# Writing out ScalarE's and VectorE's programs for the middle experts in a mixture-of-experts kernel

## The reference

```python
# x: (128, 64, 256), cond: (128, 256), weight: (256, 256), w1: (8, 256, 1024), w2: (8, 1024, 256)
ys = cond * scale
d = rsqrt(einsum('bi,io->bo', ys * ys, weight * weight) + EPS)
hidden = einsum('bsi,io->bso', x * ys[:, None, :], weight) * d[:, None, :]
logits = hidden @ wr.T                                # 8192 x 8
vals, idx = top_k(logits, 2); gating = softmax of the two
# the first 2560 tokens of each expert are kept, in order (cap)
h = gelu(einsum('ecd,edf->ecf', hidden[dispatch], w1) + b1)
y = einsum('ecf,efd->ecd', h, w2) + b2
out = x + segment_sum(y * gate, token)
```

## Time and profile before

| | |
|---|---|
| median of 3 runs | 928.7 us (927.84 to 929.36) |
| the profiled execution's own time | 929.16 us |
| its span, first to last instruction | 927.0 us |
| busy: TensorE | 903.6 us, 97% of the span |
| busy: ScalarE, VectorE, GpSimd | 543.0, 486.7, 436.4 us |
| mean granted TensorE clock | 0.992 of full speed |

### The profile page before, as it was taken

The page is one execution under the profiler, slowest core; times in us unless marked ns, Lnnn a source line. Parts: engine busy times, 40 slices in busy tenths (PEclk is TensorE's granted clock), DMA queues, the critical chain, the costliest instruction groups (busy, mean ns, idle before and its releaser), DMA issues.

```text
span 927.0 us, 20314 instructions
## 1 busy us (share of the span) xinstructions
PE 903.6 (97%) x6627; PEld 866.5 (93%) x6627; DVE 486.7 (52%) x1166; ACT 543.0 (59%) x1292; POOL 436.4 (47%) x472
## 2 busy tenths in 40 slices
PE   9999999999999999989999999989999999999995
PEld 6666799999999999989999999989999999999995
DVE  6589867546455554435444554435444644544442
ACT  4888655646566665656556665655566655664552
POOL 0000324555466555654446645654466544674453
PEclk9999999999999999999999999999999999999998
DMA  9675492543523353333523442333334231342232
GB/s 344 230 251 185 154 314 36 95 95 48 130 46 59 53 138 46 52 60 45 132 39 50 69 125 46 61 55 94 73 52 60 52 51 29 57 66 40 47 46 25
DMA packets 56119, 84.53 MB, mean 91 GB/s; under 512 B 6848, under 2 KB 45264, under 8 KB 55664
## 3 DMA queue, kind: packets, MB, share of 16 engines
q0 software_dynamic: 28592, 38.20, 26.9%
q1 hardware_dynamic: 25760, 44.87, 14.2%
q10 hardware_dynamic: 1696, 0.58, 0.2%
HBM read 53.71 MB, written 38.31 MB: 99 GB/s over the span
## 4 chain that ended last, share of the span: by engine, by line
PE 92%; issue 3%; ACT 2%; DVE 2%; DVEq 0%; ACTq 0%; POOLq 0%; POOL 0%
PE bank L609 13%; PE bank L623 13%; PE bank L625 13%; PE bank L626 13%; PE bank L610 13%; PE bank L611 13%; PE bank L512 5%; PE bank L597 3%; PE bank L525 2%; PE bank L527 1%; PE bank L560 1%; PE bank L492 1%; ACT sb_x L755 0%; ACT sb_h_hi L823 0%; ACT sb_hid_t L791 0%
## 5 line engine op out<-in xcount | busy, mean ns | idle before, releaser
L823 ACT ACTIVATE sb_h_raw<-bank,sb_b_now 128x384 f32<-128x384 f32 (+1 forms) x416 | 223.4, 537 | 257.6 <-PE bank L611 240.1
L1232 DVE TENSOR_TENSOR sb_h_lo<-sb_h_raw,sb_h_hi 128x384 fp32r<-128x384 f32 (+1 forms) x416 | 213.3, 513 | 280.5 <-ACT sb_h_hi L823 264.6
L623 PE MATMUL bank<-sb_w_hi,sb_h_hi 128*128 128x256 f32 x1064 | 305.2, 287 | 1.2 <-DVE sb_h_lo L1232 1.2
L436 POOL DMA_INDIRECT out_rows<-sb_y,sb_add_ids x154 | 254.2, 1650 | 102.0 <-issue 51.8
L625 PE MATMUL bank<-sb_w_lo,sb_h_hi 128*128 128x256 f32 x1064 | 300.2, 282 | 0.0
L626 PE MATMUL bank<-sb_w_hi,sb_h_lo 128*128 128x256 f32 x1064 | 298.9, 281 | 0.0
L609 PE MATMUL bank<-sb_xt_hi,sb_w_hi 128*128 128x384 f32 (+1 forms) x832 | 265.9, 320 | 7.7 <-ACT sb_h_hi L823 7.7
L611 PE MATMUL bank<-sb_xt_hi,sb_w_lo 128*128 128x384 f32 (+1 forms) x832 | 261.8, 315 | 0.0
L610 PE MATMUL bank<-sb_xt_lo,sb_w_hi 128*128 128x384 f32 (+1 forms) x832 | 261.7, 315 | 0.0
L823 ACT ACTIVATE sb_h_hi<-bank,sb_b_now 128x384 fp32r<-128x384 f32 (+1 forms) x416 | 220.9, 531 | 0.0
L623 PEld LDWEIGHTS bank<-sb_w_hi,sb_h_hi 128*128 128x128 f32 x1064 | 200.8, 189 | 2.1 <-DVE sb_h_lo L1232 2.1
(11 more groups left out here) (144 smaller groups left out, 582.5 us busy)
## 6 DMA issues: line engine op xcount, KB each, us to landing
sb_w_raw<-in_w SPq DMA_DIRECT2D x16, 1024.0 KB
hidden<-sb_rows SPq DMA_DIRECT2D x4, 2112.0 KB, 9.5
sb_x<-in_x_t SPq DMA_DIRECT2D x16, 512.0 KB, 5.8
out_rows<-in_x SPq DMA_DIRECT2D x16, 512.0 KB, 7.0
out_rows<-sb_y,sb_add_ids POOLq DMA_INDIRECT x155, 3.7
sb_xg<-hidden,sb_gather_ids POOLq DMA_INDIRECT x133
sb_b<-in_b SPq DMA_DIRECT2D x1, 1024.0 KB, 9.9
hidden<-sb_empty SPq DMA_DIRECT2D x4, 132.0 KB, 7.8
```

Of the source, the lines that this page charges most:

```text
L436: pool.indirect_dma_start(out, bass.IndirectOffsetOnAxis(add_ids[:, s:s + 1], axis=0), y[s][:, :], None, compute_op=ALU.add,).then_inc(add ...
L623: pe.matmul(y, hi, w_hi[u][:, cols], start=(f == 0 and (s != 1 or only is not None)), stop=False, skip_group_check=True)
L823: ins = act.activation(h[:, 0:subs * P], h_bank[f % H_BANKS][:, 0:subs * P], ACT.Gelu_apprx_tanh, bias=b1_now[u][:, f:f + 1])
L1232: dve.tensor_tensor(h_lo[f % RING][:, cols], h_raw[f % RING][:, cols], h_hi[f % RING][:, cols].bitcast(F32), ALU.subtract).then_inc(h_read ...
```

## The change

On ScalarE and on VectorE the loop over three pairs of experts is replaced by a Python loop over the experts 1 to 6, so that each of the six has its own code, one behind the other. The hardware loops over an expert's blocks stay. `e` is now a number when the program is built and no longer a register. The other engines' programs are the same.

```diff
--- before.py
+++ after.py
@@ -852,12 +852,10 @@
             act.wait_ge(plan_ready, 1)
             _, _, end = plan_of(act, 0)
             expert(0, 0, EARLY - 1, end, end)
-            with act.Fori(0, E // 2 - 1) as pair:
-                for u in (1, 0):
-                    e = pair * 2 + (2 - u)
-                    bias(u, e)
-                    start, short_at, end = plan_of(act, e)
-                    expert(u, e, start, short_at, end)
+            for e in range(1, E - 1):
+                bias(e % 2, e)
+                start, short_at, end = plan_of(act, e)
+                expert(e % 2, e, start, short_at, end)
             bias(1, E - 1)
             start, short_at, end = plan_of(act, E - 1)
             with act.Fori(start, short_at) as b:
@@ -1302,11 +1300,9 @@
                 one_block(0, 0, b, None)
             _, _, end = plan_of(dve, 0)
             expert(0, 0, EARLY - 1, end, end)
-            with dve.Fori(0, E // 2 - 1) as pair:
-                for u in (1, 0):
-                    e = pair * 2 + (2 - u)
-                    start, short_at, end = plan_of(dve, e)
-                    expert(u, e, start, short_at, end)
+            for e in range(1, E - 1):
+                start, short_at, end = plan_of(dve, e)
+                expert(e % 2, e, start, short_at, end)
             start, short_at, end = plan_of(dve, E - 1)
             with dve.Fori(start, short_at) as b:
                 one_block(1, E - 1, b, None)
```

## The result

The changed kernel takes **915.68 us** (median of 4 runs, 915.32 to 917.48). The kernel before, on the same occasion, takes 929.03 us (4 runs, 927.84 to 929.90). The ratio is 0.9864, with a 95% interval of 0.9850 to 0.9879: 13.4 us, or 1.4%, faster. The mechanism is the one that was forecast: the profile after shows it, and e3 tests its cause. What came on top of the forecast's 11.2 us is a second matter, and has its own experiments (e4, e8 and e10).

A forecast was written before the change was run, and what follows sets the result against it. TensorE was taken as the bound, losing 11.24 us at two jumps back over the expert pair while ScalarE and VectorE refetch code. 929.16 - 11.24 = 917.92, less 0.46 to the median: 917.5 us, range 915.8 to 920.0.

The forecast's parts named there:

- TensorE pays only where it waits or has waited: TensorE, busy 903.6 of 927.0 us: ScalarE and VectorE edits matter only where it waits, or runs at lower clock afterwards.
- The jump back fetches its target: ScalarE and VectorE, jumping back over the pair twice, no longer hold the target's code and must have it brought.
- Price of the rounds, 11.24 us: Excess between TensorE's transposes at the two jumps back over 15.63 us elsewhere: 5.40 and 5.84 us, all removed.
- The upper end of 11.8: Upper end for the two rounds' price, allowing a few tenths the interval may miss; the lower end was 7.21 us.
- Written-out code costs nothing on first entry: Four more experts' code on ScalarE and VectorE: entering untouched code costs 0, as in the first pass through the pair.
- Case (1), inner loops across a border: Rival: 11 inner-loop jumps on VectorE and ScalarE across 8 KB borders each refetch, costing 30 us; 947.2 us, chance 0.03.
- Cases (2): Rival: at the two rounds only the idle time goes, other lateness keeps the rest; 921.5 us, chance 0.06.
- (3): Rival: first entry costs as much as return, a gap at each of five expert boundaries; near 928.7 us, chance 0.03.
- the sum: Whole kernel: profiled 929.16 us less 11.24 gives 917.92, less 0.46 to the median; forecast 917.5 us.
- the spread as 0.8 us either way: Scatter of the kernel before's runs shown, 927.84 to 929.36 us, taken as the forecast's own spread with a few tenths more.

The follow-up runs named there:

- e3: Kernel before with the loop over pairs kept, its first instruction placed at a block's start on ScalarE and VectorE; 916.64 us, ratio 0.9867.
- e4: The changed kernel measured again in five runs, against the kernel before; 916.28 us against 929.15, ratio 0.9878.
- e8: The changed kernel plus 27 small unread TensorE matmuls in the two pauses ahead of expert 0's first products; 915.61 us, ratio 0.9861 to the kernel before.
- e10: The kernel before, unchanged, measured and profiled a second time; 927.67 us, ratio 0.9995 to the other runs of the same kernel.
- e5: Kernel before, loop over pairs kept: ScalarE's starts at a block's start, VectorE's 100 instructions into one; 916.45 us, ratio 0.9867.
- e6: Kernel before with the loop over pairs kept and its jump back announced (hint_back_edge=True); 915.62 us, ratio 0.9865.
- e9: Kernel before, pair loop kept: VectorE's at a block's start, ScalarE's 100 instructions into one, its body 32 instructions longer; 917.79 us, ratio 0.9892.
- e2: Kernel before with only VectorE's loop over pairs written out, ScalarE's kept; 924.0 us, ratio 0.9948.
- e7: Second measurement and profile of the kernel with only VectorE's pair loop written out, against the kernel before; 924.9 us, ratio 0.9964.

## Why the prediction was right, and where it was not

- **TensorE pays only where it waits or has waited**: right. The other four expert ends and all other blocks kept their length to 0.02 us.
- **The jump back fetches its target**: right, and sharpened. It is neither the distance nor the jump (e3 keeps both and has no gap), but where the body lies: body and block ahead come to five blocks where, as I read e3, e5, e6 and e9, four are held.
- **Price of the rounds, 11.24 us**: the profiles give 11.28. This is the same profile before, so the better test is the second one, with 11.81 us. The upper end of 11.8 was about right for one profile.
- **Written-out code costs nothing on first entry**: right; TensorE is busy 700.00 of 700.00 us.
- **Case (1), inner loops across a border**: fell. On the borders that the prediction counted, expert 1's loop over short blocks crosses one in the changed program, and at its first jump back, at 271 us, VectorE does not idle at all:

```profile
270.94 0.63 DVE L1258 TENSOR_SCALAR sb_y<-sb_y,sb_gates 128x256 f32<-128x256 f32 x2
271.62 0.43 DVE L1230 TENSOR_TENSOR sb_h_lo<-sb_h_raw,sb_h_hi 128x256 fp32r<-128x256 f32 x1
272.23 0.43 DVE L1230 TENSOR_TENSOR sb_h_lo<-sb_h_raw,sb_h_hi 128x256 fp32r<-128x256 f32 x1 [0.18 <-ACT sb_h_hi L823]
```

- **Cases (2) and (3)**: fell. Nothing stood behind the pauses, and at the boundaries of experts ScalarE's opening copy has no idle time. VectorE is idle for 0.73 and 0.69 us behind "issue" at the two places, which TensorE does not feel.
- **The step that was mis-sized**: the sum took everything outside the two rounds as fixed, and the spread as 0.8 us either way. The profile before had the 1.53 us of half clock at 113 us in it, and some 0.6 us more in two small places; the profile after had none of it. The view of before had it (granted clock 0.91 from 105 to 125 us), and the earlier trace rows shows that I looked at the clock, but only at the rounds. The forecast came out 1.8 us above the first median, and its range, down to 915.8 us, held the second median and not the first.

**What stays open.** The medians differ by 13.4 us in the first comparison and 12.9 us in the second, and the rounds account for 11.3 to 11.8. The lowest run on record of the kernel before is 926.66 us and of the change 915.32 us, 11.3 us apart, which suggests that the rest lies in what varies from run to run. It would need the early stretch, or something like it, to be more frequent in the kernel before than in the change. It was so in the runs at hand (both profiles of the one, neither of the other), and I take it for chance, since nothing differs up to there and loop kernels such as e6 and e9 lack it too; that is argued and not shown.

## What to carry to other kernels

When a queue of the kind "instruction" moves several packets at once and engines idle for nothing but "issue", look for a loop whose body, with the block ahead, does not fit what the engine holds; here that was, as I read the runs, four blocks of 128 instructions on ScalarE and VectorE. Writing the loop out, placing its head at a block's start, or announcing the jump each brought back 12.5 to 13.4 us, and the last two leave the program as short as it was. Price such a stall by the interval between two marks on the engine that sets the pace, against the same interval where nothing happens; the idle times behind each engine at the stall do not give that engine's share.

## What the runs showed of the hardware that I had not expected

- Instructions for ScalarE and VectorE come in packets of 8 KB on queue 14 (23 packets, 0.19 MB in the change; 14 packets in e3), and the runs fit four such blocks held per engine (e3, e5, e6, e9). Another instruction queue moves packets of 16 KB, 37 of them (0.61 MB) in every profile; that they are TensorE's is inferred. TensorE's loops, of some 215 to 268 instructions in the built program, showed no fetch stall in any profile.
- A jump to a dropped block left VectorE idle for 3.40 and 3.20 us in e5, where 0.81 us is usual (e3), and ScalarE for 1.52 and 1.78 us in e9, for 2.33 to 3.42 us in e2, e7 and the kernel before. A border 4 instructions behind the target (2 on VectorE) went with a second gap, on ScalarE of 2.29 to 2.90 us of idle time, and by the estimate under e9 this second one made most of TensorE's pause.
- TensorE's pauses of 2.89 us and more at the rounds (before, e10, e2, e7) were each followed by a stretch at the 1.2 GHz level, mostly of 3.4 us; the one of 2.73 us in e7 was not. At 110 to 113 us two short pauses (1.0 and 0.5 us, alike in all eleven profiles without the fill) were followed by such a stretch in six of them and not in the other five.
